# Local attention on one core: a quarter's scores over half of four PSUM banks, on eight tiles of TensorE, and turned probabilities in one bank in two halves

## The reference

```python
qkv = x @ w_qkv.T + b_qkv                                  # 16 heads, q, k, v of 16 columns each
k_win, v_win = k_pad[:, :, idx, :], v_pad[:, :, idx, :]    # the 33 keys around each query
scores = jnp.einsum('bhsd,bhswd->bhsw', q, k_win) / jnp.sqrt(16.)
attn = jax.nn.softmax(scores, axis=-1)
ctx = jnp.einsum('bhsw,bhswd->bhsd', attn, v_win)
return ctx @ w_out.T + b_out                               # on layer-normed x, added to x
```

## Time and profile before

| | |
|---|---|
| runs before, median (lowest, highest) | 1608.75 us (1607.25, 1608.76) |
| profiled execution, its own time | 1606.99 us |
| its span, first to last instruction | 1605.2 us |
| mean granted clock of TensorE | 0.998 |
| PE busy, share of span | 1576.5 us, 98% |
| DVE, ACT, POOL busy | 1208.8, 966.5, 732.5 us |
| the local attention | about 1275 to 1483 us of the span |

### The profile page before, as it was taken

How to read it: one execution, slowest core, us unless ns; L and a number is a source line. 1 busy time by engine, 2 the same in 40 slices (tenths; PEclk the granted TensorE clock), 3 DMA queues, 4 the chain that set the end, 5 groups by cost and what they waited for, 6 DMA issues and landing times.

```text
span 1605.2 us, 47181 instructions
## 1 busy us (share of the span) xinstructions
PE 1576.5 (98%) x17333; PEld 1142.1 (71%) x17334; DVE 1208.8 (75%) x2549; ACT 966.5 (60%) x1816; POOL 732.5 (46%) x678
## 2 busy tenths in 40 slices
PE   8999999999999999999899999999999999998999
PEld 4665569999656767666555669999667777877676
DVE  7777777888677677768766667887688879888876
ACT  5355455777477777763434336777476676675764
POOL 2442242444256565543322333444245667777343
PEclk9999999999999999999999999999999999999999
DMA  8132233333311111003300123333433022221001
GB/s 265 59 105 91 90 99 96 117 117 118 93 28 33 34 26 26 1 1 107 102 27 27 40 80 101 117 115 112 102 67 52 2 81 75 62 69 42 27 26 53
DMA packets 91468, 115.81 MB, mean 72 GB/s; under 512 B 9456, under 2 KB 76688, under 8 KB 91344
## 3 DMA queue, kind: packets, MB, share of 16 engines
q1 hardware_dynamic: 70992, 71.21, 15.4%
q0 software_dynamic: 20352, 42.88, 9.4%
HBM read 66.14 MB, written 47.90 MB: 71 GB/s over the span
## 4 chain that ended last, share of the span: by engine, by line
PE 87%; DVE 7%; ACT 2%; issue 2%; DMA 1%; POOL 1%; SPq 0%; DVEq 0%; ACTq 0%; POOLq 0%
PE ps L2097 20%; PE ps L2099 19%; PE ps L2098 19%; PE ps L2339 3%; PE ps L2389 3%; PE ps L2390 3%; PE ps L2340 3%; PE ps L2113 2%; PE ps L2296 2%; PE ps L2629 2%; PE ps L2663 2%; PE ps L2641 1%; PE ps L2491 1%; PE ps L2451 1%; PE ps L2516 1%
## 5 line engine op out<-in xcount | busy, mean ns | idle before, releaser
L805 POOL DMA_INDIRECT routed<-work x142 | 137.1, 965 | 216.3 <-ACT work L1072 211.0
L2097 PE MATMUL ps<-xt_hi,wsh 128*128 128x512 f16 x508 | 193.4, 381 | 8.2 <-DVE work L1596 7.6
L2099 PE MATMUL ps<-xt_hi,wsh 128*128 128x512 f16 x508 | 193.4, 381 | 0.0
L2098 PE MATMUL ps<-xt_lo,wsh 128*128 128x512 f16 x508 | 193.2, 380 | 0.0
L1003 ACT ACTIVATE work<-ps 128x512 f32<-128x512 f32 x128 | 76.2, 597 | 167.7 <-PE ps L2099 167.3
L1596 DVE SCALAR_TENSOR_TENSOR work<-ps,work 128x512 f32<-128x512 f32 x128 | 88.0, 689 | 80.0 <-ACT work L1003 75.8
L2097 PE MATMUL ps<-wsh,work 128*128 128x256 f16 x512 | 139.6, 273 | 0.7 <-DVE work L1527 0.6
L2099 PE MATMUL ps<-wsh,work 128*128 128x256 f16 x512 | 139.6, 273 | 0.0
L2098 PE MATMUL ps<-wsh,work 128*128 128x256 f16 x512 | 139.6, 273 | 0.0
L1099 ACT ACTIVATE work<-ps,cols 128x512 f32<-128x512 f32 x120 | 82.6, 690 | 54.9 <-PE ps L2340 43.6
L2389 PE MATMUL ps<-w2q,work 128*128 128x256 f16 x512 | 113.4, 273 | 0.0
(11 more groups left out here) (296 smaller groups left out, 5118.9 us busy)
## 6 DMA issues: line engine op xcount, KB each, us to landing
work<-expert_x SPq DMA_DIRECT2D x142, 129.0 KB, 2.1
later<-values SPq DMA_DIRECT2D x32, 256.0 KB, 3.6
yg<-in_w_later SPq DMA_DIRECT2D x9, 498.0 KB, 3.4
w1q<-in_w_later SPq DMA_DIRECT2D x9, 498.0 KB, 3.8
yg<-in_w SPq DMA_DIRECT2D x16, 256.0 KB, 3.7
values<-wsh SPq DMA_DIRECT2D x8, 512.0 KB, 3.8
expert_x<-work SPq DMA_DIRECT2D x30, 129.0 KB, 3.2
yg<-routed SPq DMA_DIRECT2D x7, 512.0 KB, 3.7
```

The lines of the kernel that those rows point to most:

```text
L805: nc.gpsimd.indirect_dma_start(routed[:, :], bass.IndirectOffsetOnAxis(m.homes[:, i:i + 1], 0), m.t_y[:, i % 4, :], None).then_inc(s[f"til ...
L2097: nc.tensor.matmul(out_, a[0], b[0], start=start, stop=False)
L2098: nc.tensor.matmul(out_, a[0], b[1], start=False, stop=False)
L2099: return nc.tensor.matmul(out_, a[1], b[0], start=False, stop=stop)
```

## The change

Three things change in the middle sequences (`wide` and `turned_amid` say where; 24 of the 32 quarters are wide).

1. The scores of a quarter go to banks 2 to 5, 256 of 512 columns of each. Each group of 32 rows has a bank of its own, and the two matmuls of a block (f = 0 and 1) use different halves of the partitions, so that all eight tiles are used. DVE's window reads four banks; context picks the turned columns in the new order.
2. Bank 5 no longer being free, the probabilities are turned in bank 6 alone: four transposes ahead of the context, and four behind the next scores, each half waiting for the copy of the one before. ACT copies the first half where it copied both, the second behind exp (at t = 2 ahead of it).
3. The transposes of the normed tiles go to banks 2 and 3, behind the context of t = 2, and wait for that quarter's window. The next scores, which use these banks, stand behind both pieces of rows and wait for `xt_lo`. DVE does the sum of the quarter before ahead of `xt_lo`.

```diff
@@ -502,6 +502,19 @@
...
     return (1, 0, 2, 5)[j] if is_first(g) else 1 - j % 2
+WSCORE = 2
+def wide(g, t):
+    return 1 <= g < NSEQ - 1 if t else 2 <= g
+def turned_amid(g, t):
+    return 1 <= g < NSEQ - 1 if t < 2 else g < NSEQ - 2
+def turn_bank(g, t, b):
+    return 6 if turned_amid(g, t) else WTURN + b
...
     return 4 if is_last(g) and t == 2 else 7
@@ -1254,11 +1267,11 @@
             act.wait_ge(s["sub_ready"], g * TPS + t + 1)
...
-        def turned(g, t):
-            for b in range(2):
+        def turned(g, t, halves=range(2)):
+            for b in halves:
                 act.wait_ge(s["pt_ready"], (g * TPS + t) * 2 + b + 1)
                 nc.scalar.activation(m.pt[:, t % 2, 4 * b:4 * b + 4].rearrange("p a b -> p (a b)"),
-                                     ps[:, WTURN + b, :], ACT.Copy).then_inc(s["pt_copied"], 1)
+                                     ps[:, turn_bank(g, t, b), :], ACT.Copy).then_inc(s["pt_copied"], 1)
...
             act.wait_ge(s["c_ready"], g * TPS + t + 1)
@@ -1294,16 +1307,17 @@
             for t in range(TPS):
...
                     normed_rows(g)
+                g2, _, t2 = turns_back(g, u, t, 2)
+                turned(g2, t2, (0,))
+                ct_hi(*turns_back(g, u, t, 3))
                 if t == 2:
-                    xt_hi_of(g + N0(n) + 2, u, WXT_AMID)
-                if has_turn(g, t, 2):
-                    g2, _, t2 = turns_back(g, u, t, 2)
-                    turned(g2, t2)
-                if has_turn(g, t, 3):
-                    ct_hi(*turns_back(g, u, t, 3))
+                    xt_hi_of(g + N0(n) + 2, u, WSCORE)
+                    turned(g2, t2, (1,))
                 if t == 1:
...
                 exps(g, t)
+                if t != 2:
+                    turned(g2, t2, (1,))
                 if t == 0:
...
                 elif t == 1:
@@ -1959,9 +1973,15 @@
             dve.wait_ge(s["sc_ready"], g * TPS + t + 1)
...
                 dve.wait_ge(s["pt_ready"], (g * TPS + t - TPS + 1) * 2)
-            nc.vector.tensor_tensor(m.p[t].rearrange("p (j g) k -> p g j k", g=2), sc.rearrange("p (g j) k -> p g j k", g=2),
-                                    const("window")[:, None, None, :].broadcast_to([P, 2, BPT * KT, KB]),
-                                    ALU.add).then_inc(s["windowed"], 1)
+            if wide(g, t):
+                nc.vector.tensor_tensor(m.p[t].rearrange("p (b i) k -> p i b k", i=4),
+                                        ps[:, WSCORE:WSCORE + 4, 0:BPT * KB].rearrange("p i (b k) -> p i b k", k=KB),
+                                        const("window")[:, None, None, :].broadcast_to([P, 4, BPT, KB]),
+                                        ALU.add).then_inc(s["windowed"], 1)
+            else:
+                nc.vector.tensor_tensor(m.p[t].rearrange("p (j g) k -> p g j k", g=2), sc.rearrange("p (g j) k -> p g j k", g=2),
+                                        const("window")[:, None, None, :].broadcast_to([P, 2, BPT * KT, KB]),
+                                        ALU.add).then_inc(s["windowed"], 1)
             dve.wait_ge(s["windowed"], g * TPS + t + 1)
@@ -2062,10 +2082,10 @@
                     take(g - 2, lambda: sums(g - 1, 1 - u, 3))
...
                     shift(g)
-                if t == 2:
-                    xt_lo_of(g + N0(n) + 2, u, WXT_AMID)
                 if has_turn(g, t, 1) and t:
                     sums(*turns_back(g, u, t, 1))
+                if t == 2:
+                    xt_lo_of(g + N0(n) + 2, u, WSCORE)
                 if has_turn(g, t, 3):
...
                 if t == 3 and (not isinstance(g, int) or g + 3 <= NSEQ + 1):
@@ -2606,7 +2626,7 @@
             for half in halves:
...
                     pe.wait_ge(s["qk_copied"], (g + 1) * 2 * KT)
-                if half or is_first(g):
+                if is_first(g) or half and g == 1:
                     xt_ready(g + N0(n) + 1)
...
                     for k in range(KT):
@@ -2625,23 +2645,26 @@
                 for f in range(KT):
...
                     for pair in range(4):
-                        dims, out_ = slice(pair * 32, (pair + 1) * 32), slice(pair % 2 * 64, (pair % 2 + 1) * 64)
+                        dims, bank, c = slice(pair * 32, (pair + 1) * 32), 3 + pair // 2, pair % 2
+                        if wide(g, t):
+                            at, bank, c = blk * KB, WSCORE + pair % 2 * 2 + pair // 2, (pair + f) % 2
                         ins = nc.tensor.matmul(
-                            ps[out_, 3 + pair // 2, at:at + KB], m.qz[dims, u, f, t * BPT + blk].rearrange("p h q -> p (h q)"),
+                            ps[c * 64:(c + 1) * 64, bank, at:at + KB], m.qz[dims, u, f, t * BPT + blk].rearrange("p h q -> p (h q)"),
                             m.k[dims, u, f, key:key + KB], start=True, stop=True, skip_group_check=True)
...
-        def turn(g, t):
-            pe.wait_ge(s["norm_ready"], g * TPS + t + 1)
-            if has_turn(g, t, 1):
-                pe.wait_ge(s["pt_copied"], (g * TPS + t) * 2)
-            else:
-                pe.wait_ge(S[n - 1]["y_taken"], 2 * NSEQ + 2)
-            for j in range(BPT * KT):
-                ins = nc.tensor.transpose(ps[:, WTURN + j // 4, (j % 4) * P:(j % 4 + 1) * P],
-                                          m.p[t][:, 2 * j:2 * j + 2].rearrange("p a b -> p (a b)"), ident)
-                if j % 4 == 3:
-                    ins.then_inc(s["pt_ready"], 1)
+        def turn(g, t, halves=range(2)):
+            if 0 in halves:
+                pe.wait_ge(s["norm_ready"], g * TPS + t + 1)
+                if not has_turn(g, t, 1):
+                    pe.wait_ge(S[n - 1]["y_taken"], 2 * NSEQ + 2)
+            for b in halves:
+                if has_turn(g, t, 1) and (b == 0 or turned_amid(g, t)):
+                    pe.wait_ge(s["pt_copied"], (g * TPS + t) * 2 + b)
+                for j in range(4 * b, 4 * b + 4):
+                    ins = nc.tensor.transpose(ps[:, turn_bank(g, t, b), (j % 4) * P:(j % 4 + 1) * P],
+                                              m.p[t][:, 2 * j:2 * j + 2].rearrange("p a b -> p (a b)"), ident)
+                ins.then_inc(s["pt_ready"], 1)
@@ -2659,9 +2682,13 @@
                 blk, f = j // KT, j % KT
...
                     sl = slice(h * QB, (h + 1) * QB)
+                    at, from_ = j, sl
+                    if wide(g, t):
+                        at, group = blk * KT + h // 2, (f ^ h // 2) * 2 + h % 2
+                        from_ = slice(group * QB, (group + 1) * QB)
                     own = m.vz[u][:, t * BPT + blk].rearrange("p a (d e) -> p (a d) e", e=KT * 4)[:, :, f * 4 + h]
-                    ins = nc.tensor.matmul(ps[sl, context_bank(g, t), f * P + blk * QB:f * P + (blk + 1) * QB], own, m.pt[:, t % 2, j, sl],
-                                           start=True, stop=True, skip_group_check=True)
+                    ins = nc.tensor.matmul(ps[sl, context_bank(g, t), f * P + blk * QB:f * P + (blk + 1) * QB], own,
+                                           m.pt[:, t % 2, at, from_], start=True, stop=True, skip_group_check=True)
             ins.then_inc(s["c_ready"], 1)
         def project(g, u, halves=range(2)):
@@ -2744,19 +2771,24 @@
             if is_last(g):
...
             for t in range(TPS):
+                g2, _, t2 = turns_back(g, u, t, 2)
+                turn(g2, t2, (0,))
+                context(*turns_back(g, u, t, 3))
                 if t == 2:
-                    pe.wait_ge(s["qk_copied"], (g + 2) * 2 * KT - 1)
-                    transposes(g + N0(n) + 2, b=WXT_AMID)
-                if has_turn(g, t, 2):
-                    g2, _, t2 = turns_back(g, u, t, 2)
-                    turn(g2, t2)
-                if has_turn(g, t, 3):
-                    context(*turns_back(g, u, t, 3))
+                    pe.wait_ge(s["windowed"], g * TPS + t + 1)
+                    transposes(g + N0(n) + 2, b=WSCORE)
+                    turn(g2, t2, (1,))
+                    for part in range(2):
+                        rows_part(g, u, t, part)
+                    xt_ready(g + N0(n) + 2)
+                    scores(g, u, t + 1)
+                    continue
                 rows_part(g, u, t, 0)
...
                     scores(g + 1, 1 - u, 0)
+                turn(g2, t2, (1,))
                 rows_part(g, u, t, 1)
```

## The result

| | before | changed |
|---|---|---|
| runs, median (lowest, highest) | 1608.0 us (1606.54, 1608.76), 4 runs | 1620.1 us (1619.19, 1620.88), 4 runs |
| profiled execution, its span | 1606.99, 1605.2 us | 1620.66, 1618.8 us |
| mean granted clock of TensorE | 0.998 | 0.998 |

The ratio is 1.0076, with a 95% interval of 1.0059 to 1.0094: by the medians the change costs 12.1 us. The forecast was 1619, slower.

What follows compares the result with a forecast made beforehand. PE was taken to bound the middle sequences, with DVE close behind. Stalls outweigh shorter scores: +8.6 over five middle sequences and +2.0 in the second, +10.6 on 1606.99 gives 1617.6, by the runs' median 1619 us; range 1608 to 1626.

Steps and rivals of the forecast that it cites:

- What bounds the stage: Middle sequences of local attention: PE-bound, busy all 24.77 us, but DVE's take only 0.3 us of slack behind PE.
- The block of scores: PE's block of scores: eight tiles save 0.33 us, from 1.09 to 0.76, with a range of 0 to 0.46.
- 8 steps of 58 ns: Block of scores: eight tiles need 8 steps instead of 16, so at most 0.46 us is saved.
- PE's other work: Turns, contexts and rows on PE keep their number, so a middle sequence's PE work falls to about 23.3 us.
- half a turn 0.44: PE's turn of probabilities, 0.87 us whole, was counted as 0.44 for each half.
- First stall: PE ahead of the first quarter's rows, sequences three to seven: waits 2.1 us for DVE's take.
- E: Time origin within a sequence: the end of its fourth scores, from which DVE's unbroken work starts.
- Second and third stall: PE waits for ACT's copies: 0.7 us ahead of the second quarter's second half turn, 0.4 ahead of the third quarter's turn.
- The sum: Whole kernel: +1.7 us per middle sequence, +8.6 over five, +2.0 in the second sequence, 0 after the seventh; +10.6.
- PE stays the bound: Faster rival: DVE's take comes early enough, below 7.2 us, so 24 wide quarters give back 7.9: 1601 us; chance 0.09.
- Only DVE's stall: Rival: ACT's copies come in time, middle sequences of 25.36 us, +3.7 in all, 1612.5 us; chance 0.12.
- Eight tiles no faster: Rival: the block of scores stays 1.09 us, costing 3.6 us more, 1623 us; chance 0.12.

Runs made afterwards that it cites:

- e1_scores_amid: Changed kernel with the third quarter's fourth scores back between the two pieces of rows, transposes moved to the quarter's front: 1612.95 us, ratio 1.0036.
- e2_act_order: Changed kernel with ACT's second-quarter order changed: first half's copy ahead of the normed tiles, second's ahead of keys and exp: 1612.81 us, ratio 1.0033.
- e8_half_columns: Changed kernel with each matmul of a wide block of scores streaming 32 of its 64 key columns, other half left out: 1620.26 us, ratio 1.0075.
- e7_before_halves: Kernel before with probabilities turned in one bank in two halves and ACT's two copies in the changed kernel's places: 1611.80 us, ratio 1.0026.
- e6_before_moved: Kernel before with only the third quarter's fourth scores moved behind both pieces of rows: 1614.13 us, ratio 1.0036.
- e3_four_tiles: Changed kernel with the loops of a block of scores swapped, so four tiles are in use at a time: 1622.64 us, ratio 1.0095.
- e5_ct_hi_first: Changed kernel with the edits of e1_scores_amid and e2_act_order, plus ACT's ct_hi ahead of the second quarter's normed tiles: 1611.46 us, ratio 1.0023.

## Why the prediction came out right, step by step

**What bounds the stage.** Right: a shorter block alone gives nothing, since DVE and ACT stood close behind PE. e1_scores_amid and e2_act_order each take one edge away and give back about what their waits had cost.

**The block of scores.** Mis-sized: 0.25 saved, not 0.33. The term that was off is "8 steps of 58 ns" as the bound to lean on: with half the streamed columns the block is only 0.05 shorter (e8_half_columns), so a pair every 11 ns is the pace, and not the columns.

**PE's other work: "half a turn 0.44".** Mis-sized. I halved the 0.87 of the chain view, which cuts the pieces otherwise than the timeline does. From one start to the next a whole turn took 0.97 to 1.02 before (1.00 here), and all four of a sequence 3.96:

```profile
1348.75 1.07 PE L2641 MATMUL ps<-consts,work 128*128 128x128 f32 x8
1349.75 1.21 PE L2663 MATMUL ps<-work,later 128*32 128x32 f32 x64
```

The eight halves took 0.44 to 0.59 each in the changed kernel, 4.18 together. So splitting costs 0.22 in a sequence (0.17 in e7_before_halves), and a half turn is 0.52 on the mean, not 0.44. PE was busy for 24.35 where I had 23.3, and the 1.08 between 24.35 and the pieces' 23.27 split up: 0.18 that the pieces leave out already before (24.77 against 24.59), 0.32 for four longer blocks of scores, 0.22 for the split turns, and the remaining 0.36 mostly at the four waits, where the piece ahead of a wait counts as busy for 0.04 to 0.15 longer than before.

**First stall.** Right in place and mechanism: rows began at E + 9.22, predicted 9.27. PE's wait was 1.5 (0.53 for normalize, 0.94 for take), not 2.1, since PE itself came later by the dearer pieces, at E + 7.75 without its waits instead of 7.18. Up to take this makes no difference to the time, as DVE sets the moment. e6_before_moved shows it alone, e1_scores_amid its absence.

**Second and third stall.** Predicted 0.7 and 0.4, measured 0.66 and 0.42. e2_act_order shows that both go with ACT's order; e1_scores_amid and e7_before_halves show that the third also needs the transposes behind the context.

**The sum.** Predicted +1.7 for a middle sequence, measured 2.13: 2.55 of waits less 0.42 of work. Over five, 10.56 against 8.6; second sequence 2.62 against 2.0; behind the seventh -0.54 against 0. That is 12.6 against 10.6. The runs' medians differ by 12.1. That 1619 comes within 1.1 of 1620.1 is partly luck: the 10.6 was added to a median of 1608.75, and the four runs of before shown here have 1608.0.

**The rivals.** *PE stays the bound* fell: take came at E + 9.08, far above 7.2. *Only DVE's stall* fell, since ACT's two waits are there; e2_act_order is this case made. It took 1612.8, with 1612.5 as forecast, but that close a match is luck: its sequences take 25.77 instead of 25.36, and it is 5.2 above its own runs of before instead of 3.7. *Eight tiles no faster* fell: a block is 0.84 long with eight and 0.99 with four (e3_four_tiles), and that kernel took 1622.6, where this rival had 1623.

**Where the gain went.** The parts don't add up: moved scores cost 5.8 us, half turns 4.2, each alone and with four tiles (ratios 1.0036 and 1.0026), both with four tiles and the new banks 15 (1.0095). One reason is in the traces: in e7_before_halves the transposes hide ACT's second wait. What makes up the rest is not shown. Even with every order mended (e5_ct_hi_first) the kernel stays 3.3 us above before by the medians (ratio 1.0023). In its early middle sequences PE is busy for 0.49 less than before (24.28 against 24.77), so the shorter blocks keep half of their 1.0, but 0.67 of waits, mostly for normalize, take more than that; in the later ones the gaps in PE's stream come on top.

## What to carry to other kernels

Before a step on the busiest engine is shortened or moved, count for each engine that is waited for how far it is behind at every wait: here 0.3 us of slack stood between PE and DVE's take, and a move by one piece of 1.41 was enough to lose it. Splitting a step in two that share one buffer turns the copying engine's order into part of the critical path; here the mend was on that engine, and no other wait took the place of those removed (e2_act_order). Read the length of a piece from one view, before and after: pieces of the chain and pieces of the timeline are cut at different points. Price a block of small matmuls by the rate at which they start as well as by their columns.

## What the runs showed of the hardware

- On eight tiles, matmuls of 32 rows, 64 columns of weights and 64 streamed columns start every 11 ns with their loads (64 records in 0.70 us); with 32 streamed columns it is hardly faster (0.64 us).
- Eight tiles against four in the same four banks: 0.84 against 0.99 us from block to turn.
- PE can stop within a block for 0.3 to 1.0 us with nothing waited for, and in 31 cases out of 31 it went on 1.2 to 1.6 us after a piece of instructions had landed.
- Waits that are long fulfilled are not free on PE when many stand in a row: 48 between the halves of a queries piece left a gap of 1.75 us behind 3 matmuls, and 384 in a sequence cost some 17 us.
